# A selective scan on one core: half 1's input of each pair's first state made by TensorE instead of VectorE

## What is computed

```python
h = x @ fc1_w.T + fc1_b
xc, z = jnp.split(h @ in_proj_w.T, 2, axis=-1)       # 256 inner channels each
u = silu(causal_conv4(xc) + conv_b)
dt_low, Bm, Cm = jnp.split(u @ x_proj_w.T, [8, 8 + 16], axis=-1)
dt = softplus(dt_low @ dt_proj_w.T + dt_proj_b)
A = -jnp.exp(A_log)                                    # 256 channels x 16 states
def step(hstate, t):
    dt_t, B_t, C_t, u_t = t
    dA = jnp.exp(dt_t[..., None] * A)
    hstate = dA * hstate + (dt_t * u_t)[..., None] * B_t[:, None, :]
    return (hstate, jnp.einsum('bdn,bn->bd', hstate, C_t))
y = (scan(step) + u * D) * silu(z)
out = (y @ out_proj_w.T) @ fc2_w.T + fc2_b
```

## Time and profile before

| | |
|---|---|
| median of three runs | 1459.11 us |
| the profiled execution's own time | 1461.46 us |
| its span, first to last instruction | 1459.30 us |
| mean granted TensorE clock, share of full speed | 0.908 |
| mamba_in, in the span | 763 to 857 us |
| mamba_scan | 857 to 1286 us |
| mamba_out | 1286 to 1307 us |

### The profile page before, as it was taken

The page is one execution under the profiler, slowest core; times in us unless marked ns, Lnnn a source line. Parts: engine busy times, 40 slices in busy tenths (PEclk is TensorE's granted clock), DMA queues, the critical chain, the costliest instruction groups (busy, mean ns, idle before and its releaser), DMA issues. The chain is left out here.

```text
span 1459.3 us, 21367 instructions
## 1 busy us (share of the span) xinstructions
PE 1215.0 (83%) x7478; PEld 548.7 (38%) x7478; DVE 1151.0 (79%) x1366; ACT 672.7 (46%) x1057; POOL 652.0 (45%) x468
## 2 busy tenths in 40 slices
PE   4937899999899899899968767877877877866998
PEld 2412343343334354445433212322322322355565
DVE  4869899999897458675557789999999999964554
ACT  2514899899798532132226863323333333302221
POOL 2320001000112166567651269989989979920000
PEclk9956999999999899999978959989989989985999
DMA  4321112312112263234510023423433333200331
GB/s 106 120 97 38 51 52 63 102 52 77 51 39 69 51 156 112 88 111 112 114 33 0 11 90 130 130 89 128 130 118 113 119 125 118 99 28 10 65 58 44
DMA packets 75346, 120.37 MB, mean 82 GB/s; under 512 B 13246, under 2 KB 42758, under 8 KB 75254
## 3 DMA queue, kind: packets, MB, share of 16 engines
q1 hardware_dynamic: 73958, 117.83, 27.4%
q10 hardware_dynamic: 1296, 1.33, 0.3%
HBM read 105.09 MB, written 13.63 MB: 81 GB/s over the span
## 5 line engine op out<-in xcount | busy, mean ns | idle before, releaser
L638 DVE TENSOR_REDUCE att_found<-PS 128x2 f32<-128x1024 f32 (+2 forms) x288 | 333.3, 1218 | 19.5 <-PE PS L747 17.7
L1796 PE MATMUL PS<-ms_ch,ident_sb 128*128 128x512 f32 x512 | 277.0, 668 | 71.2 <-POOL ms_ch L1903 71.2
L714 ACT ACTIVATE att_prob<-PS 128x512 f32<-128x512 f32 x576 | 313.6, 596 | 46.9 <-PE PS L769 34.9
L1903 POOL TENSOR_TENSOR ms_ch<-xnT,ms_c_rows 128x1024 f32<-128x1024 f32 x128 | 303.0, 2378 | 46.3 <-PE PS L1796 25.5
L1861 DVE TENSOR_TENSOR_SCAN xnT<-ms_decay,PS 128x1024 f32<-128x1024 f32 x96 | 216.1, 2275 | 4.2
L788 PE MATMUL PS<-att_prob,att_v 128*32 128x256 f32 (+1 forms) x2560 | 185.7, 377 | 2.8 <-ACT fr_out L703 2.6
L1796 PEld LDWEIGHTS PS<-ms_ch,ident_sb 128*128 128x128 f32 x512 | 100.6, 208 | 196.2 <-POOL ms_ch L1903 106.2
L1834 ACT ACTIVATE PS<-m_dt,m_a 128x1024 f32<-128x1024 f32 x32 | 35.8, 1118 | 263.4 <-DVE xnT L1861 263.4
L747 PE MATMUL PS<-kr,qr 55*128 55x128 bf16 (+4 forms) x1152 | 121.9, 293 | 30.9 <-PEq L260 15.6
L769 PE MATMUL PS<-qr,kr 55*128 55x128 bf16 (+4 forms) x1152 | 115.9, 279 | 15.1 <-ACT att_prob L714 8.2
L1848 DVE TENSOR_TENSOR PS<-ms_dtu,PS 128x1024 f32<-128x1024 f32 x96 | 115.1, 1214 | 9.6 <-PE PS L1787 9.3
(11 more groups left out here) (222 smaller groups left out, 1679.1 us busy)
## 6 DMA issues: line engine op xcount, KB each, us to landing
ms_c_rows<-bc_rows_dram SPq DMA_DIRECT2D x64, 512.0 KB, 5.9
f_gate_row<-gate_rows_dram SPq DMA_DIRECT2D x64, 256.0 KB, 3.5
ms_b_row<-bc_rows_dram SPq DMA_DIRECT2D x32, 512.0 KB, 3.6
f_mask_row<-mask_rows_dram SPq DMA_DIRECT2D x64, 128.0 KB, 3.1
qk_parts_dram<-qkv_parts SPq DMA_DIRECT2D x48, 128.0 KB, 1.9
heads_dram<-fr_out SPq DMA_DIRECT2D x16, 256.0 KB, 2.7
f_mask_row<-mask_rows_dram SPq DMA_DIRECT2D x64, 64.0 KB, 3.3
qr<-qk_parts_dram SPq DMA_DIRECT2D x32, 96.0 KB
```

The source lines that it names most:

```text
L638: dve.tensor_reduce(found[:, :, pair, first:first + (n - 1) * step + 1:step], PS[:, bank:bank + 2, :].rearrange("p r (w n) -> p r w n", w= ...
L714: act.activation(prob[:, step % PROB_RING * GH + h, :], PS[:, SCORE_BANK + unit % SCORE_RING, :], ACT.Exp, scale=float(D) ** -0.5).then_in ...
L1796: last = pe.matmul(PS[:, Y_BANK + 2 * half + q, :], g.ident[:, :], ch[:, half, q * CH:(q + 1) * CH], start=j == 0 and not odd, stop=j == J ...
L1903: pool.tensor_tensor(ch[:, half, :], h[:, odd, half, :], c_rows[:, s % C_RING, :], ALU.mult).then_inc(ch_ready, 1)
```

## The change

For scan (0,1) of each pair, the input dt*u*B of half 1 no longer comes from a spread of B and a VectorE product. In `mamba_in` TensorE turns B to tokens on partitions (4 small matmuls a chunk), and ScalarE copies it once into `m.bt`. In `mamba_scan`, once a sequence, TensorE turns dt*u of half 1 (`turn_dtu`, 8 transposes of 128 x 128) and ScalarE copies it to `dtu_turns` (`store_turns`). For each pair ScalarE makes 8 diagonal matrices with B's values of the even state from the identity (`diagonals`), and TensorE multiplies turned dt*u with them (`make_x`, 8 matmuls of 128 x 128, straight into the two banks of half 1). The order on TensorE, ScalarE and VectorE is written anew, both `times_u` now stand before scan (1,1) of a sequence's last pair, and the weights that `mamba_in` alone uses are released before the scan, so that the new tiles have room.

```diff
@@ mamba_loads
-def mamba_loads(nc, ctx, g):
+def mamba_loads(nc, ctx, early, g):
...
+    m.bt = sb("bt", [P, NT * NS])
+
+    m.ctx = early
...
@@ mamba_in: ScalarE part0 and end
                 act.wait_ge(c_written[k], 16 * b + 16)
+                act.wait_ge(b_turned, c + 1)
...
             ahead(act, part0, softplus)
+            act.wait_ge(b_turned, 2 + NCH)
+            act.activation(m.bt[:, :], PS[:, TURN_BANK, :], ACT.Copy).then_inc(a_steps, 1)
+            act.wait_ge(a_steps, 3)
@@ mamba_in: TensorE
             pe.wait_ge(u_ready, DI * (2 + NCH))
+            pe.wait_ge(z_ready, 2 + NCH)
...
             def project_dt(b, k, c):
+                pe.wait_ge(whole_ready, c + 1)
+                for i in range(TPC):
+                    last = pe.matmul(PS[:, TURN_BANK, bass.ds(c * (TPC * NS) + i * NS, NS)], bc_whole[0:NS, k, i * P:(i + 1) * P], g.ident[0:NS, 0:NS],
+                                     start=True, stop=True)
+                last.then_inc(b_turned, 1)
                 pe.wait_ge(low_ready, c + 1)
@@ mamba_scan
+        dtu_turns, b_diag = sb("dtu_turns", [P, TB, P]), sb("b_diag", [P, TB, P])
...
+        def states(p, odd):
+
+            return 2 * p + odd + 1
@@ mamba_scan: TensorE
-            def spread(p, odd, half):
+            def spread(p, odd):
...
+            def turn_dtu(b):
+
+                pe.wait_ge(dtu_ready, DI * (b + 1))
+                if b > 0:
+                    pe.wait_ge(scanned, scans(JB * b - 1, 1, 1))
+                for i in range(TB):
+                    last = pe.transpose(PS[:, X_BANK + 2 + i // TPC, i % TPC * P:(i % TPC + 1) * P], dtu[:, 1, i * P:(i + 1) * P], g.ident[:, :])
+                    if i % TPC == TPC - 1:
+                        last.then_inc(dtu_turned, 1)
+
+            def make_x(p):
+
+                pe.wait_ge(dtu_stored, CPB * (p // JB + 1))
+                pe.wait_ge(b_diag_ready, p + 1)
+                if p > 0:
+                    pe.wait_ge(scanned, scans(p - 1, 1, 1))
+                for i in range(TB):
+                    last = pe.matmul(PS[:, X_BANK + 2 + i // TPC, i % TPC * P:(i % TPC + 1) * P], dtu_turns[:, i, :], b_diag[:, i, :],
+                                     start=True, stop=True)
+                last.then_inc(x_made, 1)
...
-            spread(0, 0, 0)
-            spread(0, 0, 1)
+            spread(0, 0)
+            turn_dtu(0)
+            make_x(0)
             for p in range(PAIRS_ALL):
-                spread(p, 1, 0)
+                if p > 0:
+                    add(p - 1, 1, 0)
+                spread(p, 1)
+                if p > 0:
+                    add(p - 1, 1, 1)
                 add(p, 0, 0)
-                if p + 1 < PAIRS_ALL:
-                    spread(p + 1, 0, 0)
-                add(p, 0, 1)
-                if p + 1 < PAIRS_ALL:
-                    spread(p + 1, 0, 1)
-                add(p, 1, 0)
                 if p % JB == SKIP_AT:
                     skip(p // JB, 0)
+                if p + 1 < PAIRS_ALL:
+                    spread(p + 1, 0)
+                add(p, 0, 1)
                 if p % JB == SKIP_AT + 1:
                     skip(p // JB, 1)
-                add(p, 1, 1)
+                if p + 1 < PAIRS_ALL:
+                    if (p + 1) % JB == 0:
+                        turn_dtu((p + 1) // JB)
+                    make_x(p + 1)
+            add(PAIRS_ALL - 1, 1, 0)
+            add(PAIRS_ALL - 1, 1, 1)
@@ mamba_scan: ScalarE
+            def diagonals(p):
+
+                n, b = 2 * p % NS, p // JB
+                if p > 0:
+                    act.wait_ge(x_made, p)
+                for i in range(TB):
+                    at = NS * (TB * b + i) + n
+                    last = act.activation(b_diag[:, i, :], g.ident[:, :], ACT.Identity, scale=m.bt[:, at:at + 1])
+                last.then_inc(b_diag_ready, 1)
+
+            def store_turns(b):
+                for k in range(CPB):
+                    act.wait_ge(dtu_turned, CPB * b + k + 1)
+                    act.activation(dtu_turns[:, TPC * k:TPC * (k + 1), :].rearrange("p j c -> p (j c)"), PS[:, X_BANK + 2 + k, :], ACT.Copy).then_inc(dtu_stored, 1)
...
+            diagonals(0)
             for p in range(PAIRS_ALL):
                 n, b = 2 * p % NS, p // JB
...
+                early_decay(p, 0, 0)
+                if p == 0:
+                    store_turns(0)
+                early_decay(p, 0, 1)
+                early_decay(p, 1, 0)
+                if p > 0 and p % JB == 0:
+                    store_turns(b)
+                if p + 1 < PAIRS_ALL:
+                    diagonals(p + 1)
 
                 act.wait_ge(scanned, scans(p, 0, 1))
@@ mamba_scan: VectorE
             for p in range(PAIRS_ALL):
                 b, j = divmod(p, JB)
-                scan_input(p, 0, 0)
-                scan_input(p, 0, 1)
+                scan_input(p, 0)
                 scan(p, 0, 0)
                 if j == 0 and b > 0:
                     gate(b - 1, 0)
                 scan(p, 0, 1)
                 if j == 0 and b > 0:
                     gate(b - 1, 1)
-                scan_input(p, 1, 0)
+                scan_input(p, 1)
                 scan(p, 1, 0)
                 if j == JB - 1 and b < B - 1:
-                    times_u(b + 1, 0)
+                    for half in range(DI):
+                        times_u(b + 1, half)
                 scan(p, 1, 1)
-                if j == JB - 1 and b < B - 1:
-                    times_u(b + 1, 1)
```

More of the change, by code:

```diff
@@ L1510, in mamba_in @@
         pool_seen = sem("pool_seen")
+        b_turned = sem("b_turned")
         whole_ready = sem("whole_ready")
@@ L1684, in _ @@
             pe.sem_inc(top_ready, 2)
+            pe.sem_inc(b_turned, 2)
             pe.wait_ge(m.loaded, m.all)
@@ L1734, in mamba_scan @@
             "diag_ready", "b_in"))
+        dtu_turned, dtu_stored, b_diag_ready, x_made = map(sem, ("dtu_turned", "dtu_stored", "b_diag_ready", "x_made"))
         c_in = g.ring_in
@@ L1778, in _ @@
         def _(pe):
-            def spread(p, odd, half):
+            def spread(p, odd):
                 n, b = 2 * p % NS + odd, p // JB
                 if odd:
-                    pe.wait_ge(scanned, scans(p, 0, half))
+                    pe.wait_ge(scanned, scans(p, 0, 0))
                 elif p > 0:
-                    pe.wait_ge(scanned, scans(p - 1, 1, half))
+                    pe.wait_ge(scanned, scans(p - 1, 1, 0))
                 for q in range(CPB):
-                    last = pe.matmul(PS[:, X_BANK + 2 * half + q, :], m.sel_b[:, n, :], m.bc[:, b * T + q * CH:b * T + (q + 1) * CH], start=True, stop=True)
+                    last = pe.matmul(PS[:, X_BANK + q, :], m.sel_b[:, n, :], m.bc[:, b * T + q * CH:b * T + (q + 1) * CH], start=True, stop=True)
                 last.then_inc(b_spread, 1)
+            def turn_dtu(b):
[15 more added lines that the diff above has]
+                last.then_inc(x_made, 1)
             def add(p, odd, half):
@@ L1825, in _, with early_decay @@
             act.preload_act_table(ACT.Exp)
+            def diagonals(p):
[10 more added lines that the diff above has]
+                    act.activation(dtu_turns[:, TPC * k:TPC * (k + 1), :].rearrange("p j c -> p (j c)"), PS[:, X_BANK + 2 + k, :], ACT.Copy).then_inc(dtu_stored, 1)
+            def early_decay(p, odd, half):
+                if p > 0:
+                    act.wait_ge(scanned, scans(p - 1, odd, half))
+                n = 2 * p % NS + odd
+                act.activation(decay[:, 2 * odd + half, :], m.dt[:, half, sequence(p // JB)], ACT.Exp, scale=m.a[:, half, n:n + 1]).then_inc(decay_ready, 1)
+            diagonals(0)
             for p in range(PAIRS_ALL):
                 n, b = 2 * p % NS, p // JB
-                for odd, half in ((0, 0), (0, 1), (1, 0)):
-                    if p > 0:
-                        act.wait_ge(scanned, scans(p - 1, odd, half))
-                    act.activation(decay[:, 2 * odd + half, :], m.dt[:, half, sequence(b)], ACT.Exp, scale=m.a[:, half, n + odd:n + odd + 1]).then_inc(decay_ready, 1)
+                early_decay(p, 0, 0)
[7 more added lines that the diff above has]
+                    diagonals(p + 1)
                 act.wait_ge(scanned, scans(p, 0, 1))
@@ L1858, in scan @@
                     dve.wait_ge(decay_ready, early(p, odd, half))
-                    dve.wait_ge(input_ready, early(p, odd, half))
+                    if half:
+                        dve.wait_ge(x_made, p + 1)
+                    else:
+                        dve.wait_ge(input_ready, states(p, odd))
                     factor, x = decay[:, 2 * odd + half, :], inputs(half)
@@ L2242, in program @@
         with ExitStack() as scope:
-            m = mamba_loads(nc, scope, g)
-            norm_transpose(nc, g, 1, [m, m.last])
-            mamba_in(nc, g, m)
+            with ExitStack() as early:
+                m = mamba_loads(nc, scope, early, g)
+                norm_transpose(nc, g, 1, [m, m.last])
```

(1 more changed line is left out.)

34 lines of the change are left out of this document (18 added, 16 removed).

## The result

The changed kernel takes **1473.92 us** (median of 4 runs, 1467.15 to 1478.38) against 1458.89 for the kernel before in the same session (4 runs, 1455.82 to 1461.19): a ratio of **1.0109, interval 1.0083 to 1.0134**. It is slower by about 15 us, where 18 us less had been forecast. Its profiled execution took 1472.87 us, with a span of 1471.1.

A forecast was written before the change was run, and what follows sets the result against it. VectorE was taken to bound the scan, GpSimd 8% behind. Scan gain -27.5, scan's end +1.4, low clock +4 and the stage ahead +4 gave -18.1: 1441.0 us from 1459.11, range 1429 to 1457.

The forecast's parts named there:

- The pair: VectorE in the scan: a pair of states takes 11.43 us instead of 12.34, as one product of three goes.
- The first x late: Start of the scan: the first sequence's second scan comes some 2.7 us later than before, awaiting dt*u, turn, copy, products.
- The scan's end: After the last scan: the last gate ends about 7.3 us later instead of 5.9, adding 1.4.
- GpSimd's pace: GpSimd in the scan: without its wait it needs 11.68 us a pair and is the next limit.
- C: Rival, chance 0.10: first scan of half 1 waits for x in every pair, 1.3 us on average, total 1483.
- D: Rival, chance 0.05: no effect because GpSimd already sets the scan's pace; 1457 us.
- The sum for the scan: Whole scan: 27.5 us gained over four sequences, less 1.4 at its end and 4 for the low clock.
- x's slack of 1.3 us: TensorE in each pair: products end 1.3 us before VectorE needs x, at the full clock, behind one addition.
- four more operations ... make 4.5: VectorE at a change of sequence: two dt*u products and two gates take 4.5 us together.
- The gate's stall: Three changes of sequence: VectorE's gate stalls 3.1 us for the queued addition; 3 in all set aside for low clock.
- rival B: Rival, chance 0.16: sequence changes and start run at 1.2 GHz, +3.5 three times, +2 at the start; 1453.5 us.
- The stage ahead: mamba_in's loop over chunks: turning B makes TensorE the bound and adds 4 us, bounds 0 to 9.

The follow-up runs named there:

- e3: The changed kernel with both skip groups placed on TensorE ahead of add(p,0,0), where it waits for GpSimd: 1463.41 us, ratio 1.0040 to the kernel before.
- e6: The changed kernel with one operand of the dt*u products at changes of sequence read from PSUM, the next spread waiting for them: 1453.20 us, ratio 0.9979.
- e8: The changed kernel with dt*u of half 1 ahead of a sequence's last scan and half 0 behind it: 1457.12 us, ratio 0.9986 to the kernel before.
- e4: The changed kernel with the old sequence's last addition of half 0 ahead of the turns of dt*u: 1456.68 us, ratio 0.9988 to the kernel before.
- e7: The changed kernel with B turned in the scan, skips moved, the old sequence's addition ahead of turn_dtu, and dt*u split: 1431.90 us, ratio 0.9826.

## Why the prediction was wrong

**Where it held.** The pair (11.43 forecast, 11.44 measured). x in time in every plain pair, products 1.95 (1.8). The diagonals hidden: eight of ScalarE's in 2.45 us (2.5). The first x late by 2.58 (2.7). The scan's end: the last gate ends 6.46 after the last scan (7.3 forecast, 5.9 before). GpSimd's pace 11.56 to 11.6 a pair (11.68). The sign was wrong, and not by the one rival that had the kernel slower: C had x late by 1.3 us in each of 32 pairs, and x is waited for nine times in the whole scan, 10.5 us in all, most of it in the skip pairs and the first one. D can be dropped too: GpSimd sets the pace only for a few pairs.

**The sum for the scan failed by 24 us.** It gave 428.8 - 27.5 + 1.4 + 4 = 406.7; measured were 430.6. From the intervals between the last scans of pairs:

1. *The skips: left out, +13.1.* The prediction worked out x's slack of 1.3 us behind "one addition", and did so for a plain pair only. Two pairs of each sequence have 1.72 us of skip in that queue, ahead of a spread or of x; they take 12.7 to 13.1 us and 13.2, not 11.44. The order stood in the diff. The slack was misjudged as well: with 1.3 us of it the skip ahead of x would have cost 0.4, and it cost 1.66. Without the skip the products would have begun at 945.99, 1.48 after the pair's start at 944.51, where the prediction had 0.2, because the addition ahead of them waits for a GpSimd that runs behind. In the plain pair above they begin 0.85 after it (909.81 against 908.96). e3 removes the waits.
2. *dt*u: "four more operations ... make 4.5", +8.6.* The change puts both products beside GpSimd's weighings. The last pair of a sequence takes 16.57, not 13.7; 2.9 three times. The price of a product was read from a row of the old place, where it had started as GpSimd sat idle or changed instructions. e6 and e8 show the cause. The Trainium skill, page "GPSIMD Engine Reference", section "8. Key points", says that GpSimd shares its SBUF interfaces with VectorE and that they contend where a VectorE instruction has two SBUF inputs. The traces agree: 5.20 with two SBUF operands, 2.33 for the pair of products with one, and GpSimd's own instruction 3.33 instead of 2.35. Every other VectorE operation in the scan has one of its two operands in PSUM.
3. *The gate's stall: 3.1 forecast, 4.4 to 5.1 measured,* +5.2 in three first pairs, against 3 set aside for the low clock there. The mechanism was as foretold, and the size wrong by the clock, in one term: at the first change the turns were over 2.17 after the pair's start (2.2 forecast) and the products began at 2.85 (2.8), but they took 3.65 at the 1.2 GHz level, not the 1.8 of the full clock. So rival B was right in kind, and about half its price (+1.4 to 2.1, not 3.5, each time; at the first change the addition behind ran at full speed again, 1.88). But its cause, the turns, is not what decides: e4 has the same turns and the full clock behind them. e4 removes the stall altogether.
4. Other small waits come to 2.1 (1 set aside), the scan's end to 0.8 less than forecast.

13.1 + 8.6 + (5.2 - 3) + (2.1 - 1) - 0.8 = 24.2, against 23.9 to be explained.

**The stage ahead: +4 forecast, +11.0 in the profile.** At the full clock the estimate was about right: 0.48 a chunk, eight chunks, 3.8, and 4.7 in e3. That is partly luck: the 0.5 came from 0.94 of TensorE's work against ScalarE's pace of 4.2, and the chunks took 3.75 before and 4.23 after, not 4.2 and 4.7. The bounds of 0 to 9 had the low clock as their top end; the choice within them was wrong, because the clock was taken from the earlier trace rows as if it would stay with a different mix of matmuls. The other five profiles with turns had 51.6 to 55.9.

Together 24 + 7 = 31 us, less about 1.5 elsewhere: from the forecast of -18.1 to the +11.4 between the two profiled executions. (Between the medians it is +15.0.) e7 closes the account the other way: with these places mended, the scan is 26.6 shorter, and the prediction had 22.1 for it. That these are near is partly chance: the 22.1 still had three gate stalls of 3.1 in it, which e7 hasn't, and e7 pays for GpSimd's pace instead.

## What to carry to other kernels

When a queue's order is changed, walk through the iterations that are not like the others (here those with a skip, and the last of a sequence): nearly all of the scan's loss lay in four of eight pairs, and none in the pair whose working the prediction rested on. A slack worked out for one pair shrinks where another engine falls behind a little in each. Price an instruction by the neighbours that it will have in its new place, not by its row in the old one. Price small matmuls that go into a stage whose tensor engine is nearly full at both clock levels.

## What the hardware showed unexpectedly

- A VectorE product with both operands in SBUF and a GpSimd product hold each other up, and the rows fit a plain order: whichever starts second waits until the other's instruction is over. In the kernel after, the first dt*u starts at 966.99, GpSimd's running weighing is over by 967.77, and the next weighing, from 967.77 on, takes 3.33 instead of 2.35, as the second dt*u has to wait for it in turn: 5.20 for the two. The longest single dt*u of the kernel after takes 3.36 us instead of 1.20. One scan between the two products shifts the second wait from VectorE to GpSimd (1.92 and 1.19, with GpSimd at 3.34 and 3.26, in e8).
- TensorE's granted clock had a mean of 0.57 while the engine was busy 32.00 of 32.00 us (829 to 861 of the kernel after). A full engine kept neither level, and the same code had a mean clock of 0.74 to 0.91 in six profiles.
- Matmuls that read 16 rows from partition 0 on and others that read 8 rows from partition 32 on overlap in the records: the turns of a chunk lie between 822.81 and 823.87, the first record of dt's projection starts among them at 823.29, and the chunk is 0.48 longer, not the 1.06 of that stretch.
